# Where a transformer block on one core makes its late modulation columns and turns its second batch's rows

## What is computed

```python
mod = (_silu(L0_c) @ L0_wmod).reshape(L0_c.shape[0], 6, 1, -1)
sa, ca, ga, sb, cb, gb = (mod[:, 0], mod[:, 1], mod[:, 2], mod[:, 3], mod[:, 4], mod[:, 5])
ga = (2 * (ga >= 0) - 1) * jnp.maximum(jnp.abs(ga), 0.25)
gb = (2 * (gb >= 0) - 1) * jnp.maximum(jnp.abs(gb), 0.25)
h = _layernorm(x, axis=-1) * (1 + ca) + sa
x = x + ga * _L0_attn_ref(h, L0_attn_Wq, L0_attn_Wk, L0_attn_Wv, L0_attn_Wo)
h = _layernorm(x, axis=-1) * (1 + cb) + sb
x = x + gb * _L0_ffn_ref(h, ...)
```

## Time and profile before

| | us |
|---|---|
| median of 3 runs | 452.83 |
| lowest and highest of them | 452.75, 453.12 |
| the profiled execution's own time | 453.68 |
| its span, first to last instruction | 451.9 |
| busy: PE, PEld, DVE, ACT, POOL | 427.8, 308.4, 360.6, 349.4, 343.4 |
| PE's mean granted clock | 0.992 |

### The profile page before, as it was taken

How to read it: one execution, slowest core, us unless ns; L and a number is a source line. 1 busy time by engine, 2 the same in 40 slices (tenths; PEclk the granted TensorE clock), 3 DMA queues, 4 the chain that set the end, 5 groups by cost and what they waited for, 6 DMA issues and landing times.

```text
span 451.9 us, 12333 instructions
## 1 busy us (share of the span) xinstructions
PE 427.8 (95%) x4509; PEld 308.4 (68%) x4509; DVE 360.6 (80%) x994; ACT 349.4 (77%) x643; POOL 343.4 (76%) x306
## 2 busy tenths in 40 slices
PE   7989999899999999999999998998979989999994
PEld 4557676687877888778788786886946444554562
DVE  5978798598898889888889998998866778545666
ACT  5688999699899899989989979989854456743441
POOL 5677999996699986769999897864416794486692
PEclk9999999899999999999999999999999989999999
DMA  8465426647142685334358332265120000000001
GB/s 291 147 212 192 141 49 189 160 134 198 26 118 59 189 222 143 94 72 138 87 135 205 105 86 72 71 189 96 25 48 0 1 1 2 0 1 0 25 23 49
DMA packets 58108, 45.13 MB, mean 100 GB/s; under 512 B 36856, under 2 KB 49600, under 8 KB 58048
## 3 DMA queue, kind: packets, MB, share of 16 engines
q1 hardware_dynamic: 57440, 43.67, 35.8%
q10 hardware_dynamic: 608, 0.66, 0.4%
HBM read 23.93 MB, written 11.54 MB: 78 GB/s over the span
## 4 chain that ended last, share of the span: by engine, by line
PE 64%; POOL 14%; DVE 6%; ACT 5%; issue 4%; DMA 4%; SPq 2%; ACTq 0%; DVEq 0%; POOLq 0%
PE ps L575 10%; PE ps L490 9%; PE ps L492 9%; PE ps L491 9%; PE ps L556 5%; PE ps L558 5%; PE ps L821 3%; PE ps L599 3%; PE ps L603 3%; PE ps L601 3%; DMA oT<-on_l 2%; POOL raw L1675 2%; POOL rot L1675 2%; PE ps L851 2%; POOL rot L1694 2%
## 5 line engine op out<-in xcount | busy, mean ns | idle before, releaser
L1024 ACT ACTIVATE prob<-prob,least 128x512 f32<-128x512 f32 (+3 forms) x256 | 122.4, 553 | 0.0
L1376 DVE CUSTOM_DVE_ANT_0 prob<-ps,causal 128x512 f32<-128x512 f32 (+3 forms) x256 | 117.4, 484 | 5.9 <-PE ps L558 4.6
L1384 DVE SCALAR_TENSOR_TENSOR pl<-ps,ph 128x512 f16<-128x512 f32 (+1 forms) x128 | 105.0, 820 | 21.4 <-ACT ph L1031 18.1
L1031 ACT ACTIVATE ph<-ps 128x512 f16<-128x512 f32 (+1 forms) x128 | 86.9, 700 | 22.8 <-PE ps L575 20.4
L575 PE MATMUL ps<-ident,prob 128*128 128x128 f32 x640 | 81.9, 274 | 0.6 <-DVE pl L1384 0.6
L556 PE MATMUL ps<-kT_h,qT 128*128 128x512 f16 (+3 forms) x256 | 76.4, 301 | 3.8 <-DVE least L1376 3.4
L575 PEld LDWEIGHTS ps<-ident,prob 128*128 128x128 f32 x640 | 69.0, 142 | 1.9 <-DVE pl L1384 1.3
L558 PE MATMUL ps<-kT_l,qT 128*128 128x512 f16 (+3 forms) x256 | 70.0, 300 | 0.0
L599 PE MATMUL ps<-vh,ph 128*128 128x65 f16 x640 | 64.9, 194 | 0.4 <-DVE pl L1384 0.4
L601 PE MATMUL ps<-vl,ph 128*128 128x64 f16 x640 | 64.9, 193 | 0.0
L603 PE MATMUL ps<-vh,pl 128*128 128x65 f16 x640 | 64.8, 193 | 0.0
(11 more groups left out here) (220 smaller groups left out, 999.5 us busy)
## 6 DMA issues: line engine op xcount, KB each, us to landing
spill<-rot SPq DMA_DIRECT2D x20, 512.0 KB, 3.2
wst<-chunks SPq DMA_DIRECT2D x30, 256.0 KB, 4.3
qT<-spill SPq DMA_DIRECT2D x15, 512.0 KB, 3.7
kT_h<-spill SPq DMA_DIRECT2D x6, 256.0 KB, 3.8
xs<-x SPq DMA_DIRECT2D x2, 512.0 KB, 5.7
oT<-wmod SPq DMA_DIRECT2D x2, 512.0 KB, 8.7
raw<-chunks SPq DMA_DIRECT2D x4, 256.0 KB, 4.5
out<-xs SPq DMA_DIRECT2D x4, 256.0 KB, 2.2
```

The source lines that it names most:

```text
L1024: act.activation(prob[:, m % 2, c], prob[:, m % 2, c], ACT.Exp, bias=least[:, m % 2, qt:qt + 1], scale=-1.0).then_inc(exp_done, 1)
L1376: ins = dve.tensor_tensor_reduce(prob[:, m % 2, at:at + w], ps[:, bank, off:off + w], causal[:, S - w:S], -1.0 / HD ** 0.5, 3.0e38, ALU.ad ...
L1384: dve.scalar_tensor_tensor(out=pl[:, m % 2, c], in0=ps[:, PT_BANK:PT_BANK + 3, :].rearrange("p a b -> p (a b)")[:, c], scalar=PROB_SCALE, ...
```

## The change

It makes modulation columns 4 to 11 in `PV_BANK`: columns 4 to 7 at the end of period -2, columns 8 to 11 at the end of period -1, with one copy by DVE at the old place of the second. Batch 1's rows are normalised one tile at a time in ACT's periods 7 to 10, after the period's exponentials and the rest. They are turned in periods 11 and 13, which moves DVE's modulation to 11 and 13, ACT's high halves to 12 and 14, and POOL's low halves to 13 and 15.

```diff
-XN2_AT, GATES_AT = (6, 8), 21
+XN2_AT, GATES_AT = (11, 13), 21
+
+ROWS_AT = 7
...
-                if m == 0 and f == 1:
-                    pe.wait_ge(mod_sb, 2)
                 wait(pe, maxed, 3 * m + f - 1)
...
                 if m == 0:
-                    pe.wait_ge(mod_sb, 3)
+                    pe.wait_ge(mod_sb, 2)
                 if m - 1 in XN2_AT:
                     pe.wait_ge(hT_ready, XN2_AT.index(m - 1) + 2)
...
             pe.wait_ge(ld_mod2, 32)
             project(16)
-            modulation_products((4,), 1)
-            project(17)
-            modulation_products((5,), 1)
-            project(18)
-            modulation_products((6, 7), 1)
-            project(19)
-            modulation((8, 9), 1)
+            for step in range(17, 20):
+                project(step)
...
                 if n + 3 < HEADS:
                     scores(n + 3, 1)
+                if n == -2:
+                    pe.wait_ge(raw_out, 2)
+                    pe.wait_ge(vl_ready, 2)
+                    modulation_products((4, 5, 6, 7), PV_BANK)
                 if n == -1:
-                    modulation((10, 11), PV_BANK)
+                    modulation((8, 9, 10, 11), PV_BANK)
...
             for i in range(6, 10):
                 tile_out(i)
-            act.wait_ge(fs["m_mean"], 2)
-            for t in range(T):
+
+            def second_rows(t):
+                act.wait_ge(fs["m_mean"], 2)
                 act.activation(xn2[:, t, :], xs[:, T + t, :], ACT.Identity, bias=nrt[:, T + t:T + t + 1],
                                scale=rstd[:, T + t:T + t + 1]).then_inc(xn_ready, 1)
...
                 if n - 1 in XN2_AT:
                     second_high(XN2_AT.index(n - 1))
+                if 0 <= n - ROWS_AT < T:
+                    second_rows(n - ROWS_AT)
...
             value_low(6)
             value_low(7)
-            modulation_out(1, slice(4, 10), 1)
...
                 if n == -1:
-                    modulation_out(2, slice(10, 12), PV_BANK)
+                    modulation_out(1, slice(4, 12), PV_BANK)
...
             def gate_sign(i):
                 gsrc, gs, gab = gate_parts(i)
-                pool.wait_ge(mod_sb, i + 2)
+                pool.wait_ge(mod_sb, 2)
```

## The result

| | before | after |
|---|---|---|
| median of runs on one chip, us | 452.98 (452.75 to 455.16, 4 runs) | 457.37 (456.26 to 459.98, 4 runs) |
| ratio, 95% interval | | 1.0087 [1.0052, 1.0122] |
| profiled execution, its own time / span, us | 453.68 / 451.9 | 456.26 / 454.3 |
| PE's mean granted clock | 0.992 | 0.991 |

The change makes the kernel slower by 0.9%, or 4 us. The forecast was 453.2 us and no change, with a range up to 455.8. The same kernel timed again beside other versions gave 457.48 us, ratio 1.0082 [1.0047, 1.0118]. Each ratio is worked out from the single fast runs and is not the quotient of two medians (here 1.0097).

A forecast was written before the change was run, and what follows sets the result against it. PE bounds most places; the start's chain and POOL's stretch to 82.7 us are exceptions. 1.34 + 0.81 - 1.11 - 1.67 + 0.98 = +0.35 us, so 453.2 us against the median, no change; range 451.6 to 455.8.

The forecast's parts named there:

- ACT's rows leave the start: 0.: Start: removing ACT's four row tiles (2.08 us) gains nothing, since `rotated_high(2)` also waits for POOL's sum; 0 us.
- Products leave the front of head 0's scores: 0.: Start: 12 fewer products on PE gain nothing, since head 1's first fill waits for its queries' transfer; 0 us.
- Rival 3: Start and period 10: earlier queries hide products (-0.8 us), or the stall goes whole (-0.73); both -1.9; chance 0.26.
- Eight products at the end of period -2: +1.34.: Start: 16 records taking 1.62 us between the queries' transfer and head 0's transposes make the start 1.34 us later.
- Four products more at the end of period -1: +0.81.: Start: DVE's copy, ahead of the second half of `probs_low(0)`, comes 0.81 us later, delaying PE's remaining transposes and `values(0)`.
- The clock in the start: PE's granted clock in the start: no term in the sum; a fall there was considered only as a rival.
- Rival 2: Start, PE from 25 to 30 us: clock falls while waiting for queries, costing 0.5 to 1.7 us; chance 0.18.
- The forecast's own sign for this: Start through period 10: the prediction called itself wrong if the clock fell anywhere before 90 us; no size given.
- POOL loses a low half in period 8: -1.11: Period 8: POOL's stretch that ACT waits for shortens, bringing `rotated_high`, `probs_high(11)` and the `output` block 1.11 us earlier.
- the clock in period 10: -1.67: Period 10: PE's stall shrinks to some 1.5 us, so the clock stays at full speed, winning 1.67 us.
- Transposes in periods 11 and 13: +0.98.: Periods 11 and 13, where PE bounds: four transposes of 0.49 us, twice, with nearly no wait for `norm`; +0.98 us.
- POOL's low halves and SP: Periods 13 and 15: POOL's idle time covers the low halves; SP issues the same transfers in the same order; both 0.

The follow-up runs named there:

- rows only: Kernel before with only batch 1's rows moved to periods 7 to 10 and turned in 11 and 13, modulation unmoved: 452.71 us, ratio 0.9968.
- twice: Changed kernel with the 12 products of columns 4 to 9 also made ahead of head 0's scores, results unused: 455.52 us, ratio 1.0041.
- few and long: Changed kernel with 11 constant matmuls of 512 columns ahead of head 0's scores: 454.48 us in one run, beside 455.43 for the kernel before.
- wide: Changed kernel with each product of columns 4 to 11 made 64 columns wide in place of 2: 455.39 us, ratio 1.0042.
- modulation only: Kernel before with only the modulation products moved to the ends of periods -2 and -1, rows and transposes unmoved: 458.26 us, ratio 1.0088.
- warm: Changed kernel with 12 constant matmuls of 512 columns in PE's two idle stretches of the start: 455.75 us, ratio 1.0039.
- the three wide versions: Wide, gap and wide, and the kernel before with later turning and all late modulation ahead of head 0's scores, products 64 columns wide (ratio 0.9914).
- gap and wide: Changed kernel with products of columns 4 to 7 ahead of the wait for head 1's queries and all products 64 columns wide: 453.27 us, ratio 0.9989.
- the first experiments: Rows only, modulation only and the changed kernel again (457.48 us), measured beside the kernel before (453.56 us).
- many and short: Changed kernel with 24 constant matmuls of 64 columns ahead of head 0's scores: 463.57 us in one run.
- turn only: Kernel before with batch 1's rows turned in periods 11 and 13, not 6 and 8, nothing else moved: 452.22 us, ratio 0.9967.

## Why the prediction was wrong

It was wrong in the start: a term put at 0 was 0.97 us, and the fall of the clock there had no term. Its range ended 1.6 us too low. By its own steps:

- **"ACT's rows leave the start: 0."** Held: rows only is level with before at periods -1 to 6.
- **"Products leave the front of head 0's scores: 0."** This is the step that failed. Its reason was that the queries' landing hangs on SP and on `rot` alone. The issues didn't move, but the landing came 0.87 us later, and head 1's fill 0.97 later. Rival 3 had expected a movement here, in the other direction.
- **"Eight products at the end of period -2: +1.34."** The mechanism held. The records took 1.76 us and not 1.62, and all of it reached the transposes. Landing and products together made L575 start at 34.11, not 33.00.
- **"Four products more at the end of period -1: +0.81."** Held: the copy waited, and period 0 came +0.66 behind what period -1 had lost.
- **The clock in the start** had no term in the sum, and this is the second failure. Rival 2, chance 0.18, had the fall and a price of 0.5 to 1.7; the price was 1.5. Its place (25 to 30 us) and its cause (the idle wait) were not those of the fall at 39.8, which went with the width of the products. The forecast's own sign for this, a fall anywhere before 90 us, came true. The fall behind the wait was there as well, in the change run again. Start in all: 0.97 + 1.76 + 0.66 + 1.50 = 4.89.
- **"POOL loses a low half in period 8: -1.11"** and **"the clock in period 10: -1.67".** Held: -2.73 in place of -2.78. The first `output` block starts 3.74 us later than before (89.83 - 86.09), which is 1.17 less than the 4.91 of period 6. From it to period 11 PE takes 1.75 us in place of 3.31, which is the clock's 1.56. ACT's wait was 0.23 us, PE's stall 1.59, and the clock stayed.
- **"Transposes in periods 11 and 13: +0.98."** +0.94, without a wait in front. POOL's low halves and SP cost nothing: step 48's period starts +3.12, like the three before it.

The sum of these is +3.12 at period 17 against +0.35 forecast. The profiled execution ended at +2.4 in span, and it was the fastest of four, whose mean clocks run from 0.991 down to 0.985. The medians lie 4.4 apart. Of the miss of 2.8, 1.0 is the landing and 1.5 the clock. The miss between the medians is 4.2 (457.37 - 453.2). The other 1.4 is about the size of one more fall: the profile of the change run again has one at 31 us and 1.6 us more at period -1. That the median run has it too wasn't traced. The landing and the clock are separate: twice and few and long took the first away and kept the second, and wide did the reverse.

## What to carry to other kernels

Work that fills a wait is worth its whole length there and costs its whole length behind the wait; before moving it, ask what else hangs on the time that it kept. Very narrow matmuls are poor filler: here they looked busy, cost the same as ones 32 times as wide (1.76 and 1.79 us for 16 records), and in six profiles the clock of what followed was halved, so try them wide where the bank has room. Judge the clock by many runs and not by one profile. And run the two halves of a change apart: here one was a gain of 0.3% hidden behind a loss of 0.9%.

## What the runs showed of the hardware

- Behind head 1's queries the granted clock went with the width of the matmuls and not with PE's busy time. Six profiles have both groups of 16 narrow records behind head 1's queries and wide work around them (the change, its second profile, modulation only, warm, twice, few and long), and in all six the clock falls within 1.5 us of the end of the second group. None of the three wide versions has a fall before 45 us. In single runs the narrow versions reach a mean clock of 0.996 at most (46 runs), wide and gap and wide reach 1.000 in 8 of 24.
- A transfer landed 0.87 us later or not, with the same issues on SP, by what PE did 3 us before. The mechanism is open.
- Mean clocks of single runs lie in steps. The kernel before, in 29 runs beside the first experiments, has clusters at 0.996 (spans near 450.7 us), 0.992 (near 452.3) and 0.988 (near 454), so about 1.6 us a step, which is the price of one fall. Its profiled execution (0.992) has two falls, in period 10 and behind the gate's narrow matmuls at about 370 us. The runs at 0.996 fit one fall less, but they were not traced, and which of the two they lack is open.
- How long it stays down differs: from 39.8 to about 43.2 us in the change, from 32 to about 49 us in many and short, with narrow work in between.
- The last stretch, from L838's wait to the end, took 9.7 us in the kernel before, rows only and turn only, and 8.9 in the change. All of the difference lies behind the issue of the last transfer, `out<-xs`: 4.6 us to the end in those three (451.9 - 447.29 before) and 3.8 to 3.9 in the other thirteen profiles (454.3 - 450.46 in the change). This is why the profiled executions end 2.4 us apart with +3.1 at the last heads. The cause is open.
